# Graph attention layer: accumulating transfers for residual and x sum, x asked for a unit ahead, and ScalarE comparing from a PSUM copy of the s1 row with 13 of 16 chunks

## The chip, the cores and the metric

The kernel runs on one core of a Trainium2 chip. The engines meant below are TensorE (PE; its weight loads are PEld), VectorE (DVE), ScalarE (ACT), GpSimd (POOL) and SyncE (SP, which here only issues transfers). The metric is the device time of one execution in microseconds (us).

## The reference

One layer of graph attention over 8 graphs of 2048 nodes, with 8 heads of 64 features, then a residual and a layer norm. x is (8, 2048, 512), adj is (8, 2048, 2048) of 0 and 1.

```python
h = einsum('bnf,hfo->bhno', x, W)
s1 = einsum('bhno,ho->bhn', h, a1);  s2 = einsum('bhno,ho->bhn', h, a2)
e = leaky_relu(s1[..., :, None] + s2[..., None, :], negative_slope=0.2)
attn = softmax(where(adj > 0, e, -9e15), axis=-1)
out = layernorm(x + concat_heads(attn @ h), axis=-1)
```

## The kernel before

exp(leaky_relu(s1+s2)) is a product of a factor of the row and one of the column on each side of zero. So a head's attention for 512 rows needs two 0/1 masks, "edge and s1+s2 > 0" (`m_pos`) and "edge and not above 0" (`m_neg`), each multiplied with h times a column factor, split into a high and a low fp16 part.

**Batch and unit.** A batch (`b`, 8 of them) is one graph. It begins with a stage of 16 chunks: PE computes h for 128 columns (L426, fp32), DVE scales and splits it (L679 to L684, in `split_chunk`), and POOL subtracts to get the low parts (L892, L894). PE may be four chunks ahead, one per bank of `H_BANKS`. Then come 32 units: blocks of 512 rows (`k`, 4) by heads (`h`, 8). A unit is 4 x (1 + 32) positive and 4 x 32 negative matmuls of 65 columns (L442 to L446, L466, L467).

**How a unit's masks come about.** SP spreads the unit's s1 row over all partitions (`load_s1`, L264). The comparisons with the 16 chunks of s2 are written to `step`: ACT makes 12 (L504, `compare`), reading the row in SBUF, DVE 4 (L693, `DVE_SLOTS`). A `step` half is single, so ACT may write a half for unit u+1 only when DVE has taken that half of unit u (`pos_made`). DVE makes `m_pos` (L708) and `m_neg` (L717), two instructions each. On DVE the order in unit u is: largest |x| of an x tile, masks of unit u+1, extra work, `take_unit(u)` (L561 to L566, which waits for PE), a part of the layer norm.

**The next batch's x.** Half of the units (`TILE_UNIT` 0, 1, 3, 4, ... 22) handle an x tile of the next batch: SP loads it (`load_x`, L283), PE transposes it (L368), ACT copies it (L484), DVE takes the maximum (L552), POOL adds it to `x_sum` (L828). Load and use stand in the same unit. adj pieces are loaded, cut to fp8 on ACT (L478) and transposed by transfer. In units 24 to 30 PE and DVE make the next batch's scores, maxima and the small mean term.

**Output.** POOL scales each unit's result into `att` (L849, L854). After a block it adds `att` to `y`, which SP loaded with x (`residual`, L862), and DVE normalises in the next block's units 1 to 3 (`ln_first_half`, `ln_statistics`, `ln_apply`). There is one `y`.

The order on each engine is the written order of its block; semaphores are the only links.

Of the kernel before, what the change touches and what calls it, by code (L numbers as in the profile page):

```python
# [42 lines left out]
DVE_SLOTS = {0: (6, 7), 1: (6, 7)}  # L43
# [17 lines left out]
def gat_kernel(nc, x, adj, W, a1, a2, out):  # L61
# [25 lines left out]
    with ExitStack() as ctx:  # L87
# [19 lines left out]
        BANK_SUM = 5  # L107
# [19 lines left out]
        att = sb("att", [P, IT, H * O], F32)  # L127
        y = sb("y", [P, IT, F], F32)
# [46 lines left out]
        y_loaded = sem("y_loaded")  # L175
        s1_stored = sem("s1_stored")
        s1_loaded = [sem(f"s1_loaded{i}") for i in range(2)]
        out_stored = sem("out_stored", free=0)
# [13 lines left out]
        x_summed = sem("x_summed", free=2)  # L192
# [17 lines left out]
        lo_made = sem("lo_made", free=1)  # L210
        x_sum_turned = sem("x_sum_turned")
# [6 lines left out]
        r_row_made = sem("r_row_made")  # L218
        step_act = sem("step_act", free=QUADS)
# [10 lines left out]
        y_made = sem("y_made", free=0)  # L230
# [27 lines left out]
        def _(sp):  # L258
# [20 lines left out]
            def load_x(xi, slot, pair):  # L279
                sp.wait_ge(x_turned, at(x_turned, xi - 1))  # L280
                sp.wait_ge(x_maxed, at(x_maxed, xi - 1))
                sp.wait_ge(x_summed, at(x_summed, xi - 1))
                sp.dma_start(x_in[slot][:], x_tiles[bass.ds(pair, 1), slot].rearrange("a p f -> (a p) f")  # L283
                             ).then_inc(x_loaded[slot], 16)
# [7 lines left out]
            def store_block(g):  # L292
                sp.wait_ge(y_normed, g + 1)
                sp.dma_start(out_blocks[bass.ds((g + NBLK) % NBLK, 1)].rearrange("a p c f -> (a p) c f"),
                             y[:].rearrange("p (c e) f -> p c (e f)", e=2)).then_inc(out_stored, 16)
# [4 lines left out]
            for i in range(JC):  # L300
                if i == 2:
# [3 lines left out]
                    for n, a in enumerate((a1, a2)):  # L305
                        sp.dma_start(att[:, n, :], a.rearrange("h o -> (h o)").partition_broadcast(P)
                                     ).then_inc(a_loaded, 16)
# [12 lines left out]
            with sp.Fori(0, B) as b:  # L320
                for k in range(KB):
                    g = b * KB + k
                    for h in range(H):
                        unit = k * H + h
                        u = g * H + h
                        if unit == UNITS - 2:
                            sp.wait_ge(s1_stored, 16 * KB * (b + 2))
                        load_s1(u + 2, h % 2)
                        for i in cuts_of(k, h)[0] + cuts_of(k, h)[1]:
# [6 lines left out]
                        if unit in TILE_UNIT:  # L336
                            t = TILE_UNIT.index(unit)
                            load_x(JC * (b + 1) + t, t % 2, ((b + 1) * (JC // 2) + t // 2) % (NBLK * IT // 2))
                        if unit == STURN_UNIT + 1:
                            store_s1(b + 1)  # L340
                        if h == 5:
                            if k:
                                store_block(g - 1)
                            else:
                                with sp.If(b > 0):
                                    store_block(g - 1)
                        if h == 6:
                            sp.wait_ge(w_abs_summed, 1)
                            sp.wait_ge(out_stored, at(out_stored, 16 * g))
                            sp.dma_start(y[:].rearrange("p (c e) f -> p c (e f)", e=2),  # L350
                                         x_blocks[bass.ds(g, 1)].rearrange("a p c f -> (a p) c f")
                                         ).then_inc(y_loaded, 16)
            store_block(NBLK - 1)
# [9 lines left out]
        def _(pe):  # L363
# [8 lines left out]
            def turn_x_sum(n):  # L372
                pe.wait_ge(x_summed, at(x_summed, JC * (n + 1)))
# [34 lines left out]
            for fc in range(FC):  # L408
                mm = pe.matmul(ps[:, 0, :], ones[:], y[:, fc, :], start=(fc == 0), stop=(fc == FC - 1))
# [7 lines left out]
            with pe.Fori(0, B) as b:  # L417
                for jc in range(JC):
                    if jc == 2:
                        pe.wait_ge(s_col_copied, b + 1)  # L420
                    if jc == 3:
                        pe.wait_ge(tiny_step, 6 * b + 1)
                    if jc >= 4:
                        pe.wait_ge(hi_d_made, b * JC + jc - 3)
# [524 lines left out]
```

## Time and profile before

| | us |
|---|---|
| median of 3 runs (3199.03 to 3208.34) | 3201.51 |
| the profiled execution | 3208.02 |
| its span, first to last instruction | 3206.2 |
| PE busy | 2753.7 |
| DVE busy | 2742.4 |
| ACT busy | 2247.7 |
| POOL busy | 970.0 |

The mean granted TensorE clock is 0.969 of full speed. A batch takes some 390 us: 322 us for its 32 units and 69 us from the end of one batch's units to the next batch's first. PE's busy time is modelled; instructions overlap by some 0.1 us on DVE and ACT, so a mean duration is longer than the step from one instruction to the next. "issue" as a releaser means that nothing in the profile explains the wait.

### The profile page before, as it was taken

Reading aid. Unit: us, or ns where it says so; the run is one execution under the profiler, and the core shown is the slowest. Engines: PE = TensorE matmul, PEld = TensorE weight load, DVE = VectorE, ACT = ScalarE, POOL = GpSimd, SP = SyncE. Lnnn points to the kernel's source line nnn. Section 1 sums busy time; section 2 is a strip of 40 time slices with the busy share of each in tenths; the row PEclk is TensorE's granted clock in tenths of the full one; section 3 lists DMA queues with packets and bytes.
Section 4 is the critical chain, followed back from the end, with each engine's and each line's share of the span. In section 5 each row is a group of like instructions: output and inputs, shape, how many; then the busy total and the mean of one; then the engine's idle time right before and its main releaser. Section 6 shows DMA issues by size and latency. Waiting matters only on the chain.

```text
span 3206.2 us, 157311 instructions
## 1 busy us (share of the span) xinstructions
PE 2753.7 (86%) x68636; PEld 2400.1 (75%) x68636; DVE 2742.4 (86%) x4210; ACT 2247.7 (70%) x3517; POOL 970.0 (30%) x1043
## 2 busy tenths in 40 slices
PE   5898899888898889988998879998799978998887
PEld 2487776878678786788857878587785878758786
DVE  4898888988889888898888989888897988889887
ACT  2488873878648886488855878468773878738885
POOL 2522216222252223422243221532216222162221
PEclk9899999999999999999999999999999999999998
DMA  5335442444414545144442545325442344423443
GB/s 158 83 96 135 123 112 70 112 131 127 130 52 118 134 123 140 38 131 120 118 134 62 133 115 127 104 79 137 122 122 80 97 128 129 109 81 109 132 126 102
DMA packets 262958, 359.19 MB, mean 112 GB/s; under 512 B 159808, under 2 KB 159808, under 8 KB 262240
## 3 DMA queue, kind: packets, MB, share of 16 engines
q1 hardware_dynamic: 262240, 348.80, 40.5%
q8 instruction: 551, 9.03, 1.2%
q14 instruction: 167, 1.37, 0.2%
HBM read 279.97 MB, written 34.14 MB: 98 GB/s over the span
## 4 chain that ended last, share of the span: by engine, by line
PE 35%; DVE 24%; issue 17%; DMA 9%; ACT 7%; SPq 5%; POOL 1%; DVEq 0%; ACTq 0%; POOLq 0%
PE ps L426 12%; DVE step L693 11%; DMA x_in<-in_x 9%; ACT step L504 7%; PE ps L445 5%; PE ps L446 5%; PE ps L467 5%; PE ps L466 5%; DVE m_neg L717 3%; SPq L276 3%; DVE m_pos L708 2%; DVE y L589 2%; DVE total L564 1%; DVE neg_part L561 1%; SPq L269 1%
## 5 line engine op out<-in xcount | busy, mean ns | idle before, releaser
L504 ACT ACTIVATE step<-s_bc,s_steep 128x512 fp8e4<-128x512 f32 x3072 | 1916.9, 714 | 558.9 <-DVE m_pos L708 479.8
L445 PE MATMUL ps<-b_hi,m_pos 128*128 128x65 f16 x16384 | 1095.7, 196 | 22.8 <-issue 22.2
L446 PE MATMUL ps<-b_lo,m_pos 128*128 128x65 f16 x16384 | 1095.0, 195 | 18.7 <-issue 18.0
L467 PE MATMUL ps<-d_lo,m_neg 128*128 128x65 f16 x16384 | 1054.7, 194 | 33.5 <-issue 33.4
L445 PEld LDWEIGHTS ps<-b_hi,m_pos 128*128 128x128 fp8e5 x16384 | 1063.0, 99 | 24.6 <-issue 24.4
L446 PEld LDWEIGHTS ps<-b_lo,m_pos 128*128 128x128 fp8e5 x16384 | 1062.6, 99 | 25.1 <-issue 24.3
L466 PE MATMUL ps<-d_hi,m_neg 128*128 128x65 f16 x16384 | 1054.9, 194 | 27.8 <-issue 27.3
L466 PEld LDWEIGHTS ps<-d_hi,m_neg 128*128 128x128 fp8e5 x16384 | 1028.4, 98 | 62.8 <-issue 61.6
L467 PEld LDWEIGHTS ps<-d_lo,m_neg 128*128 128x128 fp8e5 x16384 | 1023.2, 98 | 19.4 <-issue 17.5
L708 DVE TENSOR_TENSOR m_pos<-step,maskT 128x1024 uint32<-128x1024 uint32 x512 | 642.8, 1294 | 63.1 <-ACT step L504 30.5
L693 DVE TENSOR_SCALAR step<-s_bc,s_neg 128x512 fp8e5<-128x512 f32 x1024 | 601.3, 650 | 6.4 <-DVE s_neg L652 3.2
L717 DVE TENSOR_TENSOR m_neg<-m_pos,maskT 128x1024 uint32<-128x1024 uint32 x512 | 603.4, 1219 | 0.0
L426 PE MATMUL ps<-W_sb,xT 128*128 128x512 f32 x1024 | 467.1, 619 | 47.9 <-DVE prod_d L684 26.4
L828 POOL TENSOR_TENSOR x_sum<-x_sum,x_in 128x512 f32<-128x512 f32 x144 | 185.6, 1289 | 886.8 <-DMA x_in<-in_x 886.7
L426 PEld LDWEIGHTS ps<-W_sb,xT 128*128 128x128 f32 x1024 | 202.0, 199 | 307.3 <-issue 272.9
L849 POOL TENSOR_TENSOR den_scaled<-den_inv,bound 128x4 f32<-128x4 f32 x256 | 81.6, 319 | 898.7 <-DVE den_inv L566 821.9
L442 PE MATMUL ps<-tiny,ones_bf 128*128 128x65 bf16 x1024 | 201.1, 196 | 175.9 <-DVE m_pos L708 153.1
L478 ACT ACTIVATE adj_cut<-adj_in 128x1024 fp8e4<-128x1024 int32 x264 | 272.4, 1046 | 101.7 <-DMA adj_in<-in_adj 101.7
L484 ACT ACTIVATE xT<-ps 128x512 f32<-128x512 f32 x144 | 83.4, 579 | 241.0 <-PE ps L368 241.0
L442 PEld LDWEIGHTS ps<-tiny,ones_bf 128*128 128x128 bf16 x1024 | 101.0, 99 | 195.6 <-DVE m_pos L708 166.5
L552 DVE TENSOR_REDUCE xmax<-x_in 128x1 f32<-128x512 f32 x144 | 98.0, 681 | 163.1 <-DMA x_in<-in_x 162.8
L561 DVE TENSOR_TENSOR neg_part<-ps,r_row 128x260 f32<-128x260 f32 x256 | 108.5, 424 | 122.5 <-PE ps L467 120.9
(79 smaller groups left out, 1841.8 us busy)
## 6 DMA issues: line engine op xcount, KB each, us to landing
adj_in<-in_adj SPq DMA_DIRECT2D x266, 512.0 KB, 4.4
s_bc<-s_rows SPq DMA_DIRECT2D x258, 256.0 KB, 3.4
x_in<-in_x SPq DMA_DIRECT2D x144, 256.0 KB, 4.4
y<-in_x SPq DMA_DIRECT2D x32, 1024.0 KB, 7.1
out<-y SPq DMA_DIRECT2D x32, 1024.0 KB, 7.1
maskT<-adj_cut SPq DMA_TRANSPOSE x264, 3.7
W_sb<-in_L_gnn_W SPq DMA_DIRECT2D x4, 256.0 KB, 6.6
s_rows<-sT SPq DMA_DIRECT2D x36, 16.0 KB
```

Of the source, the lines that this page charges most:

```text
L426: mm = pe.matmul(ps[:, H_BANKS[jc % 4], :], xT[:, fc, jc * P:(jc + 1) * P], W_sb[:, fc, :], start=(fc == 0), stop=(fc == FC - 1))
L442: pe.matmul(acc, ones_bf[:], tiny[:, h, :], start=True, stop=False)
L445: pe.matmul(acc, mask, b_hi[:, j, h, :], start=False, stop=False)
L446: mm = pe.matmul(acc, mask, b_lo[:, j, h, :], start=False, stop=(j == JC - 1))
L466: pe.matmul(acc, mask, d_hi[:, j, h, :], start=(j == 0), stop=False)
L467: mm = pe.matmul(acc, mask, d_lo[:, j, h, :], start=False, stop=(j == JC - 1))
L478: nc.scalar.activation(adj_cut8[slot][:], adj_in[slot][:], ACT.Relu, scale=STEEP, saturate=False).then_inc(adj_cut, 1)
L504: ins = nc.scalar.activation(chunk(step[qd], c, 0, BLK), s1_bc[h % 2][:], ACT.Relu, bias=s2_steep[:, j, h:h + 1], scale=STEEP, saturate=False)
L693: ins = V.tensor_scalar(chunk(step[qd], c, 0, BLK).bitcast(FP8_WIDE), s1_bc[hp][:], s2_neg[:, j, h:h + 1], STEP_UP, ALU.is_gt, ALU.mult, s ...
L708: V.tensor_tensor(words(m_pos[hp][:, js, :]), words(step[qd][:]), words(mask[:, js, :]), ALU.bitwise_and).then_inc(pos_made, 1)
L717: V.tensor_tensor(words(m_neg[hp][:, js, :]), words(m_pos[hp][:, js, :]), words(mask[:, js, :]), ALU.bitwise_xor).then_inc(neg_made, 1)
L828: G.tensor_tensor(x_sum[:], x_sum[:], x_in[slot][:], ALU.add).then_inc(x_summed, 1)
```

## The change

- ACT copies each unit's s1 row into PSUM bank 5 (new wait for its own earlier comparisons, then for the copy) and its comparisons read that bank. DVE makes 3 of 16 chunks, ACT 13.
- Bank 5 is no longer free for the stage: `H_BANKS` has three banks, and PE may be three chunks ahead.
- x tiles are asked for one unit before their use (`LOAD_UNIT`), and DVE's maximum comes after the masks, not before. The tile of unit 0 is transposed before that unit's positive matmuls.
- `x_sum` and the residual are formed by accumulating transfers that POOL issues (in the first batch's setup POOL still adds). `att` and the load of `y` are gone; there are two `y`.
- A batch's last block is normalised in the next batch's stage (behind chunks 11, 12, 14) and stored at unit 2.
- Unit 0's positive matmuls wait for the last chunk's low part only at the last mask of their first group. The loops carry `hint_back_edge`.

```diff
-DVE_SLOTS = {0: (6, 7), 1: (6, 7)}
+DVE_SLOTS = {0: (6, 7), 1: (7,)}
+    LOAD_UNIT = [max(v - 1, 0) for v in TILE_UNIT]
-    H_BANKS = (6, 5, 7, 4)
+    H_BANKS = (7, 4, 6)
...
             def compare(u, h, nth):
                 act.wait_ge(s1_loaded[h % 2], 16 * (nth + 1))
+                act.sem_inc(waited[act.engine], 1)
+                act.wait_ge(step_act, at(step_act, QUADS * u))
+                nc.scalar.activation(ps[:, BANK_S1, :], s1_bc[h % 2][:], ACT.Copy).then_inc(s1_copied, 1)
+                act.wait_ge(s1_copied, u + 1)
...
-                            ins = nc.scalar.activation(chunk(step[qd], c, 0, BLK), s1_bc[h % 2][:], ACT.Relu,
+                            ins = nc.scalar.activation(chunk(step[qd], c, 0, BLK), ps[:, BANK_S1, :], ACT.Relu,
...
-            with dve.Fori(0, B) as b:
+            with nc.Fori(0, B, engines=[dve.engine], hint_back_edge=True) as b:
...
+                    for when, work in ((11, ln_first_half), (12, ln_statistics), (14, ln_apply)):
+                        if jc == when:
+                            with dve.If(b > 0):
+                                work(KB * b - 1, 1)
...
-                        if unit in TILE_UNIT:
-                            max_x(...)
...
                             make_masks(u + 1, h + 1, maskT[k % 2], g * (H // 2) + (h + 1) // 2)
+                        if unit in TILE_UNIT:
+                            max_x(...)
...
+            def add_x(xi, t, odd, pair):
+                if t > 0:
+                    pool.wait_ge(x_summed, 16 * xi)
+                G.dma_start(x_sum[:], x_tiles[bass.ds(pair, 1), odd].rearrange("a p f -> (a p) f"),
+                            accum_op=ALU.add).then_inc(x_summed, 16)
...
-            def residual(g):
-                pool.wait_ge(y_loaded, 16 * (g + 1))
+            def residual(g, par):
                 pool.wait_ge(att_made, at(att_made, UNITS // KB * (g + 1)))
-                for half in range(2):
-                    t = slice(half * IT // 2, (half + 1) * IT // 2)
-                    G.tensor_tensor(y[:, t, :], y[:, t, :], att[:, t, :], ALU.add).then_inc(y_made, 1)
+                G.dma_start(y[par][:].rearrange("p (c e) f -> p c (e f)", e=2),
+                            x_blocks[bass.ds((g + NBLK) % NBLK, 1)].rearrange("a p c f -> (a p) c f"),
+                            accum_op=ALU.add).then_inc(y_made, 16)
```

## Rows read from the trace of the kernel before

**Rows 1.** The page: busy time by engine; the chain that ended last by engine

```profile
PE 2753.7 (86%) x68636; PEld 2400.1 (75%) x68636; DVE 2742.4 (86%) x4210; ACT 2247.7 (70%) x3517; POOL 970.0 (30%) x1043
...
PE 35%; DVE 24%; issue 17%; DMA 9%; ACT 7%; SPq 5%; POOL 1%; DVEq 0%; ACTq 0%; POOLq 0%
```

**Rows 2.** Busy by window: stretch, length, engines (instructions), PE clock, DMA share, GB/s

```profile
917.30:1239.30 322.00, 280.62 (x8436) 271.35 (x8436) 281.67 (x427) 247.99 (x392) 78.28 (x93) 0.98 0.43 115
1239.30:1308.30 69.00, 60.17 (x130) 25.84 (x129) 55.98 (x92) 30.49 (x44) 40.32 (x36) 0.92 0.36 93
930.90:1227.70 296.80, 255.51 (x7648) 246.34 (x7645) 265.50 (x399) 246.83 (x389) 66.58 (x80) 0.98 0.46 123
```

**Rows 3.** Waits in 930.9 to 1227.7: who for whom, total us, times, longest

```profile
ACT step L504 <- DVE m_pos L708: 58.3, 21, 9.3
...
PE ps L442 <- DVE m_pos L708: 22.5, 13, 5.0
...
DVE xmax L552 <- DMA x_in<-in_x: 18.1, 9, 5.1
...
POOL stat_all L840 <- issue: 14.0, 1, 14.0
```

**Rows 4.** Groups on ACT, 930.9 to 1227.7: busy us, mean ns, idle before

```profile
L504 ACT ACTIVATE step<-s_bc,s_steep 128x512 fp8e4<-128x512 f32 x348 | 217.1, 713 | 58.3 <-DVE m_pos L708 58.3
L478 ACT ACTIVATE adj_cut<-adj_in 128x1024 fp8e4<-128x1024 int32 x24 | 24.8, 1043 | 0.0
L484 ACT ACTIVATE xT<-ps 128x512 f32<-128x512 f32 x15 | 8.6, 576 | 0.0
...
L492 ACT ACTIVATE e_b<-s_rel 128x128 f32<-128x128 f32 x1 | 0.3, 299 | 0.0
```

**Rows 5.** Groups on DVE, 930.9 to 1227.7, columns as before

```profile
L708 DVE TENSOR_TENSOR m_pos<-step,maskT 128x1024 uint32<-128x1024 uint32 x58 | 73.2, 1302 | 3.9 <-DVE step L693 0.2
...
L693 DVE TENSOR_SCALAR step<-s_bc,s_neg 128x512 fp8e5<-128x512 f32 x116 | 68.2, 651 | 0.4
```

**Rows 6.** DVE in order of time: start, length, what, count, wait before

```profile
925.87 0.43 DVE L561 TENSOR_TENSOR neg_part<-ps,r_row 128x260 f32<-128x260 f32 x1 [8.26 <-PE ps L467]
...
934.34 0.43 DVE L561 TENSOR_TENSOR neg_part<-ps,r_row 128x260 f32<-128x260 f32 x1
...
936.67 1.66 DVE L693 TENSOR_SCALAR step<-s_bc,s_neg 128x512 fp8e5<-128x512 f32 x4
...
954.43 2.21 DVE L589 TENSOR_SCALAR y<-y,ln_mv,ln_rstd 128x512 f32<-128x512 f32 x4
...
1079.52 6.45 DVE L693 TENSOR_SCALAR step<-s_bc,s_neg 128x512 fp8e5<-128x512 f32 x4
```

**Rows 7.** ACT in order of time

```profile
930.98 7.49 ACT L504 ACTIVATE step<-s_bc,s_steep 128x512 fp8e4<-128x512 f32 x12 [8.40 <-DVE m_pos L708]
...
1239.31 7.48 ACT L504 ACTIVATE step<-s_bc,s_steep 128x512 fp8e4<-128x512 f32 x12 [11.05 <-DVE s_neg L652]
```

**Rows 8.** A DVE wait of the whole run; the stage's last two chunks on DVE

```profile
DVE r_row L657 <- issue: 31.0, 7, 4.8
...
1302.12 0.69 DVE L679 TENSOR_TENSOR b_hi<-ps,k_b 128x512 f16<-128x512 f32 x1 [0.95 <-PE ps L426]
...
1305.55 0.69 DVE L679 TENSOR_TENSOR b_hi<-ps,k_b 128x512 f16<-128x512 f32 x1 [0.95 <-PE ps L426]
```

**Rows 9.** PE in order of time: chunk 4's start; unit 0's start

```profile
1261.05 1.22 PE L426 MATMUL ps<-W_sb,xT 128*128 128x512 f32 x1 [2.95 <-DVE prod_d L684]
...
1308.32 0.22 PE L442 MATMUL ps<-tiny,ones_bf 128*128 128x65 bf16 x1 [2.81 <-POOL b_lo L892]
```

**Rows 10.** Transfers by line, last figure issue to landing (us); the end on POOL and DVE

```profile
y<-in_x SPq DMA_DIRECT2D x32, 1024.0 KB, 7.1
...
3191.96 4.63 POOL L862 TENSOR_TENSOR y<-y,att 128x1024 f32<-128x1024 f32 x2
...
3196.63 1.29 DVE L576 BATCH_NORM_STATS2 ln_stats<-y 128x6 f32<-128x512 f32 x2 [1.01 <-POOL y L862]
```

More of the change, by code:

```diff
@@ L126, in gat_kernel @@
         wa = sb("wa", [P, FC, 32], F32)
-        att = sb("att", [P, IT, H * O], F32)
-        y = sb("y", [P, IT, F], F32)
+        y = [sb(f"y{i}", [P, IT, F], F32) for i in range(2)]
         sT = sb("sT", [P, BLK], F32)
@@ L210, in gat_kernel @@
         lo_made = sem("lo_made", free=1)
+        x_added = sem("x_added", free=2)
         x_sum_turned = sem("x_sum_turned")
@@ L318, in _ @@
             load_s1(1, 1)
-            with sp.Fori(0, B) as b:
+            with nc.Fori(0, B, engines=[sp.engine], hint_back_edge=True) as b:
                 for k in range(KB):
@@ L325, in _ @@
                         u = g * H + h
+                        if unit == 2:
+                            with sp.If(b > 0):
+                                store_block(g - 1, 1)
                         if unit == UNITS - 2:
@@ L328, in _ @@
                         load_s1(u + 2, h % 2)
+                        for t in range(JC):
+                            if LOAD_UNIT[t] == unit == 0:
+                                load_x(JC * (b + 1) + t, t % 2, ((b + 1) * (JC // 2) + t // 2) % (NBLK * IT // 2))
                         for i in cuts_of(k, h)[0] + cuts_of(k, h)[1]:
@@ L408, in _ @@
             for fc in range(FC):
-                mm = pe.matmul(ps[:, 0, :], ones[:], y[:, fc, :], start=(fc == 0), stop=(fc == FC - 1))
+                mm = pe.matmul(ps[:, 0, :], ones[:], y[0][:, fc, :], start=(fc == 0), stop=(fc == FC - 1))
             mm.then_inc(w_abs_summed, 1)
@@ L443, in _ @@
                             for j in range(JC):
+                                if unit == 0 and it == 0 and j == JC - 1:
+                                    pe.wait_ge(lo_made, at(lo_made, 2 * JC * (b + 1) - 1))
+                                    pe.sem_inc(waited[pe.engine], 1)
                                 mask = chunk(m_pos[hp], j, it * P, P).bitcast(FP8_WIDE)
@@ L449, in _ @@
                             pe.wait_ge(lo_made, at(lo_made, 2 * JC * (b + 1)))
-                        if unit in TILE_UNIT:
+                        if unit and unit in TILE_UNIT:
                             t = TILE_UNIT.index(unit)
@@ L518, in _ @@
             compare(0, 0, 0)
-            with act.Fori(0, B) as b:
+            with nc.Fori(0, B, engines=[act.engine], hint_back_edge=True) as b:
                 for k in range(KB):
@@ L809, in _ @@
                         for when, work in ((1, ln_first_half), (2, ln_statistics), (3, ln_apply)):
-                            if h == when:
-                                if k:
-                                    work(g - 1)
-                                else:
-                                    with dve.If(b > 0):
-                                        work(g - 1)
-            ln_first_half(NBLK - 1)
-            ln_statistics(NBLK - 1)
-            ln_apply(NBLK - 1)
+                            if h == when and k:
+                                work(g - 1, (k - 1) % 2)
+            ln_first_half(NBLK - 1, 1)
+            ln_statistics(NBLK - 1, 1)
+            ln_apply(NBLK - 1, 1)
         @block.gpsimd
@@ L887, in _ @@
                 G.tensor_copy(bound[:], bound_next[:]).then_inc(bound_taken, 1)
+                with pool.If(b > 0):
+                    residual(KB * b - 1, 1)
                 for jc in range(JC):
```

136 lines of the change are left out of this document (65 added, 71 removed).

## The prediction, made before the changed kernel had run

> **What bounds the kernel now.** I read the page first, then busy time by window, the waits of one stretch, the groups on each engine there, and the engines in order of time. The page [rows 1] names no single bound: PE and DVE are both busy for 86% of the span, ACT for 70%, and the chain passes through PE, DVE, "issue", transfers and ACT. So one has to go by stretch. In the batch that I looked at, the units take 322 us and the way from the last unit to the next batch's first unit 69 us [rows 2]. I take this batch for all eight.
>
> Inside the units I took 930.9 to 1227.7, from the first comparison of unit 3 to the last of unit 31: 29 units in 296.8 us, 10.2 us each. DVE is busy for 265.5 of them, PE for 255.5, ACT for 246.8 [rows 2]. DVE's idle time is mostly 18.1 us of waiting for an x tile; PE waits 22.5 us for `m_pos`, and ACT waits 58.3 us for DVE to take a `step` half [rows 3]. So both others wait for DVE, and DVE waits for x. DVE bounds the units. It also runs slowly there: four chunks of `step` take 1.66 us when POOL is quiet and 6.45 us while POOL adds a residual and an x tile [rows 6]; over the stretch a chunk costs 68.2/116 = 0.59 us against 0.41.
>
> **The change, part by part.** I go engine by engine over the 29 units.
>
> DVE: 29 chunks fewer and the rest at about 0.45 us (POOL keeps its two small operations a unit): 87 x 0.45 = 39 for 68.2 [rows 5], so -29. `m_pos` comes down from 73.2 to 58 x 1.14 = 66.5 (1.14 is the step of undisturbed ones), -6.5. The layer norm of block 3 moves to the stage, about -5. The x waits, 18.1, go: the tile is asked for a unit (9 us or more) earlier, and is looked at after the masks. DVE's work comes to 265.5 - 40.5 = 225 us.
>
> PE: nothing is removed. Two takes that follow PE directly are 8.47 us apart [rows 6], in units with a tile; its busy time of 255.5 is what it needs.
>
> ACT: what does a comparison from PSUM cost? No row has one. A cut of 1024 elements from SBUF takes 1.043 us, an exponential of 128 takes 0.299 [rows 4]: 0.83 ns an element and 0.19 fixed, so 0.619 for 512. The copy of an x tile from PSUM, 512 elements, takes 0.576, or 0.04 less. A comparison takes 0.713 (it has a bias column), and 12 take 7.49 [rows 7], a step of (7.49 - 0.713)/11 = 0.616. Bounds: 0.616 if PSUM gives nothing, 0.576 if it gives those 0.04. I take 0.576, since the copy of x is the nearest row that reads PSUM.
>
> The new copy of s1 has 0.62 at most as its own length (same size, from SBUF); it can't overlap the comparison before it, and the next one waits for it: I take 0.75, bounds 0.6 and 1.0. It is free only while ACT would have waited for DVE anyway; that cover (58.3 us now) is what the faster DVE takes away. So I count it whole. Per unit: 13 x 0.576 + 0.75 = 8.24 us, against 7.39 now. Over the stretch: 29 x 8.24 = 239.0; 24 cuts at a step of 0.95, 22.8; 14 copies of x at 0.48, 6.7; scores and exponentials, 1.1. Sum 269.6 us. ACT becomes the bound, with PE (255.5) close behind and DVE (225) clear.
>
> Does ACT ever wait for DVE then? Count from the end of a unit's comparisons. DVE does the second `m_pos` and both `m_neg` (3.5 us), at worst a maximum (0.6), the take (1.05), the longest piece of layer norm (2.2, [rows 6]), three chunks (1.3 to 1.6) and the next first `m_pos` (1.2): done at about 10.2 us. ACT needs it for the unit after next, at 9.3 us plus cut and copy, so 11. It just fits. PE has lumps in units 24 to 27 (scores and mean, some 9 us together) and random stops. I add 5 us of lost time, bounds 0 and 20. The stretch: 274.6 for 296.8, so **-22.2 us a batch**.
>
> Before the stretch, comparison 3 waits for `m_pos` of unit 2. DVE comes to it 0.6 (maximum moved) and 0.4 (one chunk) sooner: -1.0. Behind it, ACT waits for the next batch's s2 the 11.05 us wait of [rows 7]; there the copy comes after that wait, +0.75.
>
> The boundary. DVE starts the next batch 4.7 us after its last instruction with "issue" as the reason, 31.0 us in seven times [rows 8]: it is the loop's way back. I take it that the hint removes it: -31 in all, bounds -31 and 0. It is on the path, since PE's fifth chunk waits for DVE's first [rows 9]. The three banks make PE wait for that same event with three chunks done, not four. PE needs 3.43 a chunk (DVE's last two chunks, both waiting for PE, start that far apart, [rows 8]), DVE 2.4 (four operations, each 0.6 to the next) plus its inserts; following both through the 16 chunks, with 5.4 us of layer norm now behind chunks 11, 12 and 14, DVE ends 48.4 us after its first chunk, where it now ends 46.9 (1261.05 to 1305.55 plus 2.4, [rows 8, 9]). So +1.5. Unit 0 no longer waits for the last low part before its first matmul (2.81 us idle, [rows 9]) but some 1 us into it: -1.4. Together nil, bounds -2 and +4.
>
> The transfers. A plain load of 1 MB lands in 7.1 us [rows 10]. The residual is issued after the take of unit 7, and DVE first reads it two units of some 9.4 us later: hidden, and dearer only if it takes over 18. The one place without cover is the end: POOL's addition starts at 3191.96, DVE's second half follows at 3196.63 and ends at 3197.9 [rows 10]. With 8.1 us for the transfer (7.1 and about 1 for issuing it) and 2.5 us for both halves that becomes 3202.4: +4.5. POOL's additions of x (hidden now) become issues, at no cost as long as POOL keeps a unit ahead of DVE.
>
> The Trainium skill has a rule against this (SBUF — State Buffer, Who interferes with whom): VectorE in a two-port mode locks GpSimd out of the shared port pair for the whole instruction, and only transfers that GpSimd issues suffer, since it must write their descriptors. The trace shows the same lock from the other side (6.45 for 1.66 us, above). By that rule the new transfers start later, by about one VectorE instruction; the 18 us of cover make that nothing in the sum.
>
> **Sum**, against the profiled execution of 3208.0: 8 x (-22.2 - 1.0) = -185.6; 7 x 0.75 = +5.3; -31; +4.5. That is -206.8, so 3001 us; the median stands 6.5 us below the profiled execution, so **2995 us**.
>
> **Rivals.**
> 1. PSUM saves nothing on a comparison. For: the one row that reads PSUM on ACT has another form, no bias column and a wide output. Then a step is 0.616, 29 x 13 x 0.04 = +15.1 a batch, 121 in all: 3116 us.
> 2. The three engines don't interlock as neatly: ACT goes on waiting for DVE or PE, 20 us a batch and not 5. For: it fits by only 1 us in the worst unit, and now it waits 58.3. Against: DVE gets 40 us lighter. 8 x 15 = +120: 3115 us.
> 3. ACT reads PSUM faster than I take it, and PE is the bound: the stretch falls to PE's 255.5 plus 5, -14 a batch: 2883 us. For it a comparison would have to step at about 0.54.
> 4. Slower than before: POOL is held at each transfer. It now stands idle for 14.0 us without a releaser ahead of its one odd instruction, the reduction over partitions [rows 3], so a change of kind of work can be dear there. If each of the 16 tile transfers cost it 14, it would need 16 x 15 + 8 x 1 = 248 us for 24 units in which ACT needs about 24 x 9.4 = 226, and with a like price for the way back (28 a transfer) 472 us: +246 a batch, about 4960 us. `take_unit` waits for POOL's result of two units before, so there is one unit of cover and no more. It decides from a hold of (226 - 24)/16 = 12.6 us a transfer, and the whole gain is lost from 26 us a batch more, at 14.3.
> 5. The change doesn't do what it says: the hint leaves the way back at 4.4 us. 3026 us.
>
> **From cases to numbers.** Forecast and its small variants 0.50 (2940 to 3060), rival 5 by itself 0.10, rival 1 0.13, rival 2 0.12, both together 0.03 (3116 + 120 = 3236), rival 3 0.06, rival 4 0.06. A measurement of this kernel can tell about 0.3% from no change. Slower: rival 4 but for a hold near 14 us (0.05), and most of the two together (0.02), 0.07. Same: what is left of these, 0.02. Faster: the rest, 0.91. The range leaves out rival 3, rival 4, the two together, and some edges of the others: 2925 to 3125.
>
> **What would show each step.** ACT busy for over 90% of the units, its waits for `m_pos` under 10 us in a stretch of 29 units, and the step of a comparison 0.576: the ACT term. Chunks on DVE at about 0.45 us, no wait of the maximum on x: the DVE term. The wait of L657 gone: the hint. First chunk to last split 48 us: the stage. DVE's statistics waiting for `y` only at the end: the transfers' cover. It is wrong if a comparison from PSUM costs 0.61 or more, or if DVE waits for POOL's results.

## The result, and the profile after

The changed kernel took 3148.4 us (median, 3138.4 to 3158.8) against 3200.3 (3190.6 to 3208.3) for the kernel before on the same chip: a ratio of 0.983, 95% interval 0.981 to 0.986. It is faster, by 52 us (1.7%) and not by the 205 of the forecast, and lies outside the range.

The page after, beside [rows 1]: busy time by engine, the chain that ended last by engine, and two rows of the DMA queues, GpSimd's (q0) and that of TensorE's instructions (q8) (queue, kind: packets, MB, share of 16 engines).

```profile
PE 2744.1 (87%) x68636; PEld 2398.0 (76%) x68636; DVE 2522.8 (80%) x3954; ACT 2419.3 (77%) x4029; POOL 827.5 (26%) x1011
...
q0 software_dynamic: 27136, 67.12, 12.7%
q8 instruction: 545, 8.93, 1.2%
...
PE 67%; issue 13%; DVE 10%; ACT 7%; DMA 1%; SPq 1%; POOL 0%; DVEq 0%; ACTq 0%; POOLq 0%
```

TensorE now carries the chain, with 67% for 35%; ScalarE, forecast as the bound, has 7%. Below is the batch of [rows 2]: its units, its boundary, and the 29 units from comparison 3 to comparison 31 (same columns).

```profile
892.06:1208.97 316.91, 279.15 (x8432) 270.01 (x8432) 254.32 (x393) 267.71 (x452) 59.03 (x88) 0.98 0.55 126
1208.97:1275.05 66.08, 58.28 (x132) 25.62 (x133) 56.52 (x96) 32.22 (x50) 41.22 (x35) 0.95 0.45 112
907.00:1197.20 290.20, 254.94 (x7670) 246.14 (x7669) 235.43 (x358) 265.76 (x446) 50.84 (x76) 0.98 0.58 131
```

The 29 units take 290.2 us for 296.8; 274.6 had been forecast. DVE lost 30 us of work (forecast 40), ACT took on 19 (forecast 23), and PE's 255 stayed. So PE was idle for 35.3 us (290.2 - 254.9), before for 41.3. What it waited for has changed. First the groups on PE in this stretch after, then in [rows 3]'s stretch before (busy us, mean ns, idle ahead of them, releaser):

```profile
L455 PE MATMUL ps<-b_lo,m_pos 128*128 128x65 f16 x1856 | 124.0, 195 | 12.2 <-issue 12.0
L454 PE MATMUL ps<-b_hi,m_pos 128*128 128x65 f16 x1856 | 124.0, 195 | 7.1 <-issue 7.1
L476 PE MATMUL ps<-d_lo,m_neg 128*128 128x65 f16 x1866 | 121.3, 195 | 7.1 <-issue 7.0
L475 PE MATMUL ps<-d_hi,m_neg 128*128 128x65 f16 x1866 | 121.1, 195 | 6.8 <-issue 6.7
L448 PE MATMUL ps<-tiny,ones_bf 128*128 128x65 bf16 x116 | 22.5, 194 | 2.1 <-issue 2.1
```

```profile
L445 PE MATMUL ps<-b_hi,m_pos 128*128 128x65 f16 x1856 | 125.1, 196 | 3.0 <-issue 2.9
L446 PE MATMUL ps<-b_lo,m_pos 128*128 128x65 f16 x1856 | 125.0, 196 | 0.5 <-issue 0.5
L466 PE MATMUL ps<-d_hi,m_neg 128*128 128x65 f16 x1856 | 117.8, 193 | 4.0 <-issue 3.9
L467 PE MATMUL ps<-d_lo,m_neg 128*128 128x65 f16 x1856 | 117.8, 194 | 1.4 <-issue 1.4
L442 PE MATMUL ps<-tiny,ones_bf 128*128 128x65 bf16 x116 | 22.9, 197 | 22.7 <-DVE m_pos L708 22.5
L368 PE MATMUL ps<-ident,x_in 128*128 128x128 f32 x56 | 8.9, 282 | 9.1 <-DMA x_in<-in_x 9.1
```

The idle time ahead of L442 and L368, nearly all waits for `m_pos` and for x, was 31.8 us. Ahead of the same two matmuls after (L448, and L368 with 0.0) it is 2.1, none of it for either. But the idle time inside the runs of matmuls, where nothing of the kernel is waited for, went from 8.9 to 33.2 us. I call these stops. Over the whole run the page gives them, as idle time ahead of the four mask matmul lines, as 102.8 us before and 260.1 after. With "issue" as the reason it is 100.9 and 235.2. Of the rest, in the changed kernel and all built on it, 17.4 us or so is unit 0's wait for its last low part, which in the kernel before stands ahead of L442. Two stops, in order of time, and two of the transfers that were issued, by GpSimd, some 10 us ahead of the first:

```profile
967.76 1.24 POOL L882 DMA_DIRECT2D y<-in_x  x1 [0.99 <-POOL y L876]
968.67 1.27 POOL L849 DMA_DIRECT2D x_sum<-in_x  x1
...
978.95 0.20 PE L475 MATMUL ps<-d_hi,m_neg 128*128 128x65 f16 x1 [2.23 <-issue]
...
1025.34 0.20 PE L455 MATMUL ps<-b_lo,m_pos 128*128 128x65 f16 x1 [3.12 <-issue]
```

What is waited for there is TensorE's own code. Its queue moved 8.93 MB in 545 packets of 16 KB (above), which is 65 bytes for each of its 2 x 68636 instructions, one packet for some 126 matmuls with their weight loads. The 27 stops over 0.25 us of this stretch are 126 or 127 matmuls apart, or a multiple of that, and over the run they come back at the same places of the loop's body: 13 places have one in at least seven of the eight batches. By the packet records each stop ends 1.2 to 1.6 us after the last such packet landed: the one at 1025.34 had its packet from 1022.94 to 1023.82, the one at 978.95 from 976.62 to 977.57. With no stop and at full clock PE runs through a packet's code in some 3.86 us. A packet takes about 1.0 to arrive and 1.4 more pass before PE goes on, so it has to start within some 1.45 us of PE's passing the boundary of the block before. With the boundaries laid out from the places of the stops, packets start about 1.4 us behind them in the kernel before, in the mean, and 1.9 in the changed one; some 205 of 512 start later than 1.45, and some 287 in the changed kernel.

The Trainium skill (Runtime: NRT & Kernel Launch, Instruction fetch mechanics) says that an engine's code comes in 16 KiB blocks of 256 instructions over a DMA queue of its own, the next one during the current one, at a cost that is mostly hidden. The block size agrees with these rows; the cost doesn't: 235 us of 3137 stand open.

Other rows answer to the prediction's steps. The groups of the comparison and of the DVE chunk in the stretch:

```profile
L519 ACT ACTIVATE step<-ps,s_steep 128x512 fp8e4<-128x512 f32 x377 | 221.4, 726 | 38.6 <-DVE m_pos L722 34.5 <-ACT ps L510 4.1
...
L707 DVE TENSOR_SCALAR step<-s_bc,s_neg 128x512 fp8e5<-128x512 f32 x87 | 43.8, 559 | 1.0 <-issue 0.3
```

In order of time, a unit's comparisons, and PE at the boundary (beside [rows 9]):

```profile
961.52 7.63 ACT L519 ACTIVATE step<-ps,s_steep 128x512 fp8e4<-128x512 f32 x13 [0.28 <-ACT ps L510]
...
1226.87 1.22 PE L429 MATMUL ps<-W_sb,xT 128*128 128x512 f32 x1 [7.24 <-DVE prod_d L698]
```

Waits of the whole run, then the residual's row among the issues:

```profile
DVE xmax L567 <- DMA x_in<-in_x: 25.5, 11, 7.3
...
DVE r_row L671 <- issue: 4.3, 7, 0.7
```

```profile
y<-in_x POOLq DMA_DIRECT2D x32, 1024.0 KB, 10.4
```

### The profile page after: what moved, and what is told of

It is laid out like the page before. It is cut to its first block, busy times and chain, and to the rows that moved or that the text cites. A ratio compares the mean times of both kernels' runs of the same rounds, so it can differ in the third digit from the quotient of the medians.

```text
span 3136.7 us, 158793 instructions
## 1 busy us (share of the span) xinstructions
PE 2744.1 (87%) x68636; PEld 2398.0 (76%) x68636; DVE 2522.8 (80%) x3954; ACT 2419.3 (77%) x4029; POOL 827.5 (26%) x1011
## 3 DMA queue, kind: packets, MB, share of 16 engines
q0 software_dynamic: 27136, 67.12, 12.7%
q8 instruction: 545, 8.93, 1.2%
## 4 chain that ended last, share of the span: by engine, by line
PE 67%; issue 13%; DVE 10%; ACT 7%; DMA 1%; SPq 1%; POOL 0%; DVEq 0%; ACTq 0%; POOLq 0%
PE ps L475 14%; PE ps L476 14%; PE ps L455 13%; PE ps L454 13%; PE ps L429 8%; ACT step L519 7%; PE ps L368 2%; DVE m_neg L731 1%; DVE y L603 1%; PE ps L386 1%; PE ps L399 1%; DVE prod L695 1%; PE ps L448 1%; DVE prod_d L698 1%; DVE m_pos L722 1%
## 5 line engine op out<-in xcount | busy, mean ns | idle before, releaser
L519 ACT ACTIVATE step<-ps,s_steep 128x512 fp8e4<-128x512 f32 x3328 | 1954.1, 726 | 289.7 <-DVE m_pos L722 246.9
L475 PE MATMUL ps<-d_hi,m_neg 128*128 128x65 f16 x16384 | 1071.9, 195 | 67.0 <-issue 61.2
L476 PE MATMUL ps<-d_lo,m_neg 128*128 128x65 f16 x16384 | 1072.7, 195 | 42.3 <-issue 42.1
L476 PEld LDWEIGHTS ps<-d_lo,m_neg 128*128 128x128 fp8e5 x16384 | 1039.1, 99 | 34.9 <-issue 33.3
L722 DVE TENSOR_TENSOR m_pos<-step,maskT 128x1024 uint32<-128x1024 uint32 x512 | 623.8, 1242 | 163.4 <-ACT step L519 130.6
L429 PE MATMUL ps<-W_sb,xT 128*128 128x512 f32 x1024 | 464.1, 615 | 61.5 <-DVE prod_d L698 54.7
L707 DVE TENSOR_SCALAR step<-s_bc,s_neg 128x512 fp8e5<-128x512 f32 x768 | 391.1, 565 | 12.4 <-DVE s_neg L666 3.6
L487 ACT ACTIVATE adj_cut<-adj_in 128x1024 fp8e4<-128x1024 int32 x264 | 291.1, 1132 | 120.0 <-DMA adj_in<-in_adj 120.0
L493 ACT ACTIVATE xT<-ps 128x512 f32<-128x512 f32 x144 | 96.9, 673 | 175.8 <-PE ps L368 175.8
L510 ACT ACTIVATE ps<-s_bc 128x512 f32<-128x512 f32 x256 | 174.6, 682 | 71.9 <-DVE s_neg L666 71.4
L876 POOL TENSOR_TENSOR y<-total,den_scaled 128x256 f32<-128x256 f32 x256 | 206.2, 805 | 22.7 <-POOL den_scaled L871 2.3
L448 PE MATMUL ps<-tiny,ones_bf 128*128 128x65 bf16 x1024 | 199.0, 194 | 11.2 <-issue 6.3
L917 POOL TENSOR_TENSOR d_lo<-prod_d,d_hi 128x512 f16<-128x512 f32 x128 | 176.2, 1376 | 9.0
## 6 DMA issues: line engine op xcount, KB each, us to landing
y<-in_x POOLq DMA_DIRECT2D x32, 1024.0 KB, 10.4
```

The lines of the kernel that those rows point to most:

```text
L429: mm = pe.matmul(ps[:, H_BANKS[jc % 3], :], xT[:, fc, jc * P:(jc + 1) * P], W_sb[:, fc, :], start=(fc == 0), stop=(fc == FC - 1))
L448: pe.matmul(acc, ones_bf[:], tiny[:, h, :], start=True, stop=False)
L475: pe.matmul(acc, mask, d_hi[:, j, h, :], start=(j == 0), stop=False)
L476: mm = pe.matmul(acc, mask, d_lo[:, j, h, :], start=False, stop=(j == JC - 1))
L487: nc.scalar.activation(adj_cut8[slot][:], adj_in[slot][:], ACT.Relu, scale=STEEP, saturate=False).then_inc(adj_cut, 1)
L519: ins = nc.scalar.activation(chunk(step[qd], c, 0, BLK), ps[:, BANK_S1, :], ACT.Relu, bias=s2_steep[:, j, h:h + 1], scale=STEEP, saturate= ...
```

## The experiments

Three numbers are given for each kernel: its time, as a ratio to the kernel before timed beside it (whose medians were 3193 to 3203); the stops, read from its page as above; and two stretches from the first matmul of a unit (L448) to another's, meaned over the batches: unit 3 to unit 31 (28 units), and unit 31 to the next batch's unit 3. Stops and stretches come from one execution of each kernel, and executions of one kernel differ by up to 38 us: the profile of a_extra_sp, c_split and c_best, for instance, is their slowest execution, that of the changed kernel and c_split_fine their fastest. The first experiments have the changed kernel as their base, those with b_ the kernel before, those with c_ the base named.

| kernel | median | ratio (95%) | stops | units | boundary |
|---|---|---|---|---|---|
| before | | 1 | 102.8 | 289.1 | 100.2 |
| after | 3148.4 | 0.983 (0.981, 0.986) | 260.1 | 278.1 | 101.9 |
| a_small_adj | 3045.8 | 0.954 (0.951, 0.957) | 99.4 | 263.9 | 104.1 |
| a_pool_sum | 3087.0 | 0.966 (0.960, 0.972) | 158.3 | 271.0 | 102.6 |
| a_extra_sp | 3123.6 | 0.972 (0.967, 0.978) | 223.5 | 277.8 | 102.2 |
| a_extra_pool | 3092.2 | 0.964 (0.962, 0.967) | 193.4 | 272.8 | 102.3 |
| a_sbuf_compare | 3152.8 | 0.988 (0.984, 0.991) | 270.4 | 280.9 | 101.1 |
| a_no_hint | 3134.3 | 0.979 (0.976, 0.982) | 258.8 | 275.7 | 106.1 |
| b_psum | 3208.6 | 1.004 (1.003, 1.006) | 81.6 | 284.9 | 105.7 |
| b_x_ahead | 3119.7 | 0.974 (0.972, 0.976) | 124.1 | 278.6 | 99.0 |
| b_x_psum | 3122.1 | 0.975 (0.973, 0.976) | 129.2 | 272.4 | 105.6 |
| b_x_hint | 3105.8 | 0.970 (0.967, 0.974) | 136.1 | 279.5 | 96.9 |
| b_banks3 | 3225.6 | 1.010 (1.007, 1.012) | 80.3 | 286.7 | 104.0 |
| c_fine_adj | 3080.7 | 0.963 (0.958, 0.969) | 133.1 | 268.7 | 104.2 |
| c_split | 3073.4 | 0.960 (0.957, 0.963) | 169.7 | 269.9 | 103.1 |
| c_split_sbuf | 3101.5 | 0.969 (0.966, 0.972) | 153.0 | 272.2 | 103.6 |
| c_split_fine | 3070.7 | 0.962 (0.957, 0.966) | 101.7 | 266.1 | 103.4 |
| c_ps_small_adj | 3048.9 | 0.953 (0.951, 0.955) | 87.4 | 265.5 | 103.9 |
| c_ps_small_sbuf | 3032.2 | 0.948 (0.946, 0.950) | 93.9 | 263.3 | 103.2 |
| c_best | 3080.5 | 0.963 (0.961, 0.966) | 139.9 | 271.5 | 101.9 |

**Is the code late because of the kernel's own transfers?** Of all data, the adj pieces are the most. The first experiment makes them small and leaves every instruction.

```diff
-                adj_in[slot][:], adj_tiles[..., slot * JH * P:(slot + 1) * JH * P]
+                adj_in[slot][:, 0:n], adj_tiles[..., slot * JH * P:slot * JH * P + n]   # n = 64 in the loop
```

In the loop the masks then come from stale columns.

> The changed kernel, but in the loop each adjacency transfer fetches 64 of 1024 columns (32 KB for 512 KB); the cut and transposed pieces are otherwise stale, so the masks are wrong in part. Theory 1 (TensorE's own code, which comes in 16 KB transfers over the same DMA engines, arrives late because data transfers are queued before it): TensorE's waits with the reason 'issue' inside the units, some 280 us in the changed kernel, fall under 140, and the time falls by 100 to 200 us, to 2950 to 3050. Theory 2 (TensorE at full pace outruns the delivery of its code whatever else is moved): the waits stay over 240 and the time within 40 us of 3148.

The stops fell to 99.4 us, and the ratio by 0.029, as the first theory had it. Two rows of its page, GpSimd's queue and the chain:

```profile
q0 software_dynamic: 27136, 67.12, 13.3%
...
ACT 41%; PE 29%; issue 16%; DVE 11%; DMA 1%; ACTq 1%; SPq 1%; POOL 1%; DVEq 0%; POOLq 0%
```

With the code in time ScalarE carries most of the chain (41%), as forecast, and the units take 25.2 us a batch less than before, where the prediction's stretch had 22.2. Units pass faster than in the changed kernel and the stops still go, so it is the traffic that makes them; pace alone does not. The cut on ScalarE also waited less for its pieces (78 us for 120), which is a part of the gain I can't separate.

A part of the gain comes through PE's clock. Two stretches of 127 matmuls in the changed kernel, the first between the stop that ends at 971.11 (1.92 us long) and the one that ends at 978.95, the second behind a stop of 0.60 us (columns of [rows 2]):

```profile
971.20:976.70 5.50, 5.50 (x127) 5.39 (x126) 1.48 (x2) 5.35 (x10) 0.00 (x0) 0.69 1.04 208
...
1018.20:1022.20 4.00, 4.00 (x127) 3.89 (x127) 3.41 (x8) 4.00 (x8) 0.86 (x2) 1.00 0.96 350
```

Behind the long stop PE runs partly at 1.2 GHz (granted clock 0.69 in the mean) and takes 5.5 us for what takes 4.0 at 2.4 GHz. It isn't so behind every stop: the one of 3.12 us at 1025.34 is not followed by it. Over the run the clock was 0.965 to 0.969 in the changed kernel's executions and 0.972 to 0.977 in those of a_small_adj, and PE's busy time for the same matmuls fell from 2744.1 to 2708.2 us. That is some 36 of the 93 to 103 us between the two. That the stops bring the clock down is not shown by itself.

**Which transfers of the change?** Its new kind is the accumulating one. The next kernel adds x on GpSimd again and leaves the residual's transfer as it is.

```diff
-                            add_x(JC * b + t, t, t % 2, ...)
+                            add_first_x(JC * (b + 1) + t, t % 2, (b + 1) * (JC // 2) + t // 2)
```

> The changed kernel with the x sum added up on GpSimd from the loaded tile, as before; the residual remains an accumulating transfer. Theory 1: 32 MB of 360 are no longer moved, so the waits for code fall by a tenth to a fifth and the time by 15 to 50 us. Theory 3 (it is the accumulating transfers of GpSimd's queue that hold the code up): 128 of 160 of them are gone, the waits fall by half and the time by 80 us or more. Theory 2: no change, or slower by up to 20 us since VectorE's comparisons run beside GpSimd's additions again.

Two more put the same 256 KB back beside it, without adding: once from SP, once from GpSimd.

```diff
+                            sp.dma_start(x_extra[:], x_tiles[...])       # a_extra_sp
+                            G.dma_start(x_extra[:], x_tiles[...])        # a_extra_pool
```

> a_pool_sum (sum of x on GpSimd's engine) with the 256 KB x tile loaded once more, as a plain transfer of SP's queues at the unit where the changed kernel accumulates it: the same bytes from memory as the changed kernel, no accumulation. If bytes in flight at the code's fetches count alone: back at 3140 to 3160, and TensorE's stops summed over the run back near 290 us. If the accumulating kind or the GpSimd queue counts: stays near a_pool_sum's 3087, within 15 us.

> The same extra 256 KB load, issued by GpSimd (its software-made queue), plain and not accumulating. If the queue of GpSimd is what holds the code up: near the changed kernel (3135 to 3160) while a_extra_sp stays low. If only accumulating transfers do: both stay near 3087. If bytes do: both near 3150.

a_pool_sum gains 55 us on the changed kernel (0.983 to 0.966) and its stops fall by 102; the time lies between what the two theories had said, 15 to 50 us and 80 or more. The same bytes from GpSimd's queue cost nothing that can be measured (0.964 beside 0.966), though the stops grow by 35 us. From SP's queue the ratio is 0.972, some 20 us more than a_pool_sum with intervals that touch, and 26 more than a_extra_pool; the stops grow by 65 us in its slowest execution, and neither number expected for it came (3123.6 us). So plain bytes count too, between nothing and some 40 us, and more from the queue of SP than from GpSimd's; why is open. The accumulating transfer costs 0.983 - 0.964, some 60 us, against the same bytes in the same queue: that part is the accumulation. The page shows what is different about it. First the row of a_extra_pool for this queue and for the transfer, then the changed kernel's row for the transfer:

```profile
q0 software_dynamic: 18944, 67.12, 9.4%
...
x_extra<-in_x POOLq DMA_DIRECT2D x128, 256.0 KB, 3.5
```

```profile
x_sum<-in_x POOLq DMA_DIRECT2D x128, 256.0 KB, 4.6
```

For the same 67.12 MB the queue's packets hold the engines for 12.7% of the span and not 9.4%; without either it is 6.0% (a_pool_sum). A tile's accumulation therefore takes the engines twice the time of a plain load (6.7 against 3.4 points) and lands in 4.6 us for 3.5 (the plain one of SP's queue, issued at another moment, in 4.5). The Trainium skill (DMA: Bandwidth & Descriptors, Issuing engines are not separate DMA queues) has all transfers interleaved on the same 16 engines whoever starts them. These runs agree: adj pieces from SP's queue and x tiles from GpSimd's both delay the packets of TensorE's code.

**Can the delivery be made milder?** Both from a_pool_sum: adj in four transfers of 256 columns each, and the residual in two of 512 KB, a unit apart, with the layer norm a unit later; c_split_fine has both.

```diff
+                for part in range(0, JH * P, JH * P // 4):                # c_fine_adj
+                    sp.dma_start(adj_in[slot][:, part:part + 256], ...)
-            residual(g, par)                                              # c_split
+            residual(g, par, half)    # y[par][:, 2 * half:2 * half + 2, :]
```

> a_pool_sum with each adj piece loaded in four transfers of 128 KB, so 1 KB of each row in place of 4 KB. If a code block of 16 KB waits behind single large packets in a queue, smaller packets let it through: 20 to 60 us less than 3087, TensorE's stops below 120 us. If it waits for bytes and not for packets: within 10 us of 3087; more issues on SP may even cost 5 to 20 us.

> a_pool_sum with the residual's accumulating transfer of 1 MB cut into two of 512 KB, a unit apart, and the normalization a unit later. If long accumulating transfers hold the code up: 10 to 25 us less than a_pool_sum. If the sum of accumulated bytes does: the same within 8 us.

> c_split with the adj pieces in four transfers of 128 KB each: both milder deliveries together. c_split stood at 3073 and c_fine_adj at 3081 against a_pool_sum's 3087. If shorter packets and shorter accumulations both count: 3055 to 3070. If the two differences were run-to-run spread: 3070 to 3090.

c_fine_adj took 25 us off the stops and 0.003 off the ratio, less than its interval and than the 20 us that would have told. c_split has the lowest ratio of the kernels that do the whole work, 0.960, but its interval touches a_pool_sum's, and its stops did not fall. Together they bring the stops to 101.7 and the units to 266.1 us, but that is the fastest of four executions (3056.7 to 3089.5) beside c_split's slowest, and the median is c_split's: this step stays unclear. All three beat both the kernel before and the changed one.

**Do adj and the accumulation act through the same stops?**

> a_pool_sum with each adj load in the batch loop cut from 512 KB to 32 KB (the masks are then made from stale columns; the work of the engines is unchanged): both known sources of the late code taken away. a_small_adj gained 103 us and a_pool_sum 61 over the changed kernel. If they act through the same stops of TensorE: 3010 to 3030, with the stops summed below 80 us. If the accumulating x_sum costs in another way than the code's delay: the two gains add in full, below 2990.

a_pool_sum with the small adj loads took 3048.9 us, where a_small_adj, which accumulates, took 3045.8. Neither number expected came (3010 to 3030, or below 2990). The accumulation costs 60 us with full adj loads and nothing with small ones, so the two don't add. That fits one path, the code's delay, with room for either alone. It fits as well that the engines themselves stand at 3030 to 3050 us and hide the rest: with stops at 87 to 99 us no kernel here was faster, and ScalarE, PE and VectorE share the chain. The runs don't part the two.

**What is comparing from PSUM worth?** Taken out of the changed kernel, whose stage keeps its three banks, and put alone into the kernel before:

```diff
-DVE_SLOTS = {0: (6, 7), 1: (7,)}                                        # a_sbuf_compare
+DVE_SLOTS = {0: (6, 7), 1: (6, 7)}
-                nc.scalar.activation(ps[:, BANK_S1, :], s1_bc[h % 2][:], ACT.Copy)
-                ... nc.scalar.activation(chunk(...), ps[:, BANK_S1, :], ACT.Relu, ...)
+                ... nc.scalar.activation(chunk(...), s1_bc[h % 2][:], ACT.Relu, ...)
```

> The changed kernel with comparisons from SBUF, no copy to PSUM, and 12 of 16 chunks on ScalarE, as before. If TensorE and its code bound the changed kernel (theories 1 to 3), the split of the chunks matters little: within 40 us of 3148. If ScalarE bounds it as I forecast, ScalarE loses 0.24 us a unit of work (8.24 to 7.39 plus nothing for the copy) and the kernel gets faster or stays; if VectorE is the nearer bound, it gets slower by 256 x 0.45 = 115 us.

> The kernel before with only this part of the change: s1 copied to PSUM, comparisons from there, 13 and 3 chunks, three banks in the stage. VectorE bounds the kernel before, and loses 0.59 us a unit: by that alone 256 x 0.59 = 150 us less, 3050. With theories 1 or 2, part of what TensorE no longer waits for VectorE comes back as waits for code: 40 to 100 us less, 3100 to 3160.

Neither showed a gain; b_psum missed both numbers and was slower by 13 us (0.004). Its granted clock was 0.961 to 0.966 (mean 0.964) where the kernel before beside it had 0.965 to 0.975 (mean 0.970), and PE was busy 16 us longer for the same matmuls (2770.1 for 2753.7). The late code might have hidden the gain, and in b_psum the waits for x. So x was asked for ahead in the kernel before, without and with it:

```diff
+    LOAD_UNIT = [max(v - 1, 0) for v in TILE_UNIT]
-                        if unit in TILE_UNIT: load_x(...)
+                            if LOAD_UNIT[t] == unit: load_x(...)         # and max_x after make_masks
```

> The kernel before with one part of the change: x tiles are asked for a unit ahead and VectorE takes their maximum after the masks; both sums still by accumulating on GpSimd's engine as before. If the waits for x (VectorE's 18 us in the stretch of rows 3) were the bound: some 70 to 110 us faster than before (3090 to 3130). If TensorE's pace is set by its own code arriving late (as the comparison of a_small_adj says), only the room that this leaves: 0 to 40 us faster (3150 to 3190).

> x asked for ahead and the compare from PSUM with 13 and 3 chunks, without the accumulating transfers, the two y tiles and the loop hint of VectorE's and GpSimd's loops. If ScalarE's compare was the next bound: 3000 to 3080. If the code delivery is, it stands at 3100 to 3170, and no slower than the changed kernel by more than 20 us, since it has fewer bytes in flight but no second y tile.

Asking for x ahead is worth 0.026, more than the whole change. That is the first of the two numbers expected (3090 to 3130): the waits for x were a bound, and late code took back little (stops 102.8 to 124.1). PSUM beside it is worth nothing in the time, but the table shows two halves: the units 6.2 us a batch shorter (278.6 to 272.4), the boundary 6.6 longer. The row copy takes a PSUM bank from the stage of projections, so that one edit was tried alone:

```diff
-    H_BANKS = (6, 5, 7, 4)
+    H_BANKS = (7, 4, 6)                                                  # b_banks3; waits moved to match
```

> The kernel before with one edit: the projections of the stage go through three PSUM banks in place of four (bank 5 left unused, as the row copy leaves it). From one tiny-row matmul of unit 31 to that of unit 3 of the next batch the kernel before takes 100.2 us and before + compare from PSUM 105.7. If the missing bank is what costs this, 30 to 50 us over the seven boundaries and the first: 3230 to 3250. If it is the row copy or ScalarE's longer compare in the stage: within 10 us of the kernel before.

31 us slower (30 to 50 expected), with the boundary 3.8 us longer and PE waiting for DVE there:

```profile
PE ps L426 <- DVE prod_d L684: 48.5, 8, 8.2
...
PE ps L426 <- DVE tiny_f L631: 5.3, 1, 5.3
```

The kernel before has 26.4 us in the first of these and none in the second; the changed kernel has 54.7 and 5.4. So the missing bank is 3.8 of the 5.5 us that b_psum adds at the boundary and of the 6.6 of b_x_psum, more than half of why the gain in the units doesn't show. And with the code in time?

> c_ps_small_adj with the compare back in SBUF (12 chunks on ScalarE, 4 on VectorE, no copy of the s1 row to PSUM). With the late code out of the way ScalarE's bound should show: if the compare from PSUM is worth what the prediction gave it (10 us a batch of 296.8 to 286 or less), this is 20 to 80 us slower than c_ps_small_adj. If TensorE's pace alone sets the units: within 10 us of it.

> c_split with the compare from SBUF, 12 and 4 chunks. In the changed kernel this part was worth 4 us and beside b_x_ahead nothing. If ScalarE becomes the bound as the stops get shorter: 10 to 30 us slower than c_split's 3073. If TensorE bounds: within 8 us.

> c_split_fine (sum of x on GpSimd, the residual accumulated in two halves, adj in four transfers) with the compare from SBUF again, 12 and 4 chunks, and the bank that this frees given back to the stage (four banks). If the compare from PSUM gains in the units what it costs in the stage: within 15 us of c_split_fine's 3071. If the fourth bank gives back 5 us a batch and ScalarE isn't the bound: 3030 to 3055. If ScalarE's SBUF compare bounds as in c_split_sbuf: 3065 to 3085.

c_ps_small_sbuf came out 17 us faster than its twin with PSUM, on the other side of what was expected. The chains by engine of c_ps_small_adj, then of c_ps_small_sbuf:

```profile
PE 32%; ACT 31%; DVE 17%; issue 16%; DMA 1%; ACTq 1%; SPq 1%; POOL 0%; DVEq 0%; POOLq 0%
```

```profile
DVE 33%; PE 31%; issue 21%; ACT 9%; DMA 1%; DVEq 1%; POOL 0%; ACTq 0%; POOLq 0%; SPq 0%
```

From PSUM, ScalarE's unit is 7.63 us for 13 chunks and about 1 for the copy and the wait behind it, against 7.5 for 12 from SBUF. The change moves 0.5 us off DVE and puts 1.1 on ScalarE; it trades one bound for another of much the same size. Yet c_split_sbuf was 28 us slower than c_split. A part of that came with a lower clock (0.962 to 0.968 for 0.970 to 0.972, PE busy for 2747.3 us and not 2725.3); why PE had less of it there, and why the order turns, is open. c_best, with the fourth bank back, took 1.7 us a batch off the boundary of c_split_sbuf, and with the finer adj some 17 us off its time (0.969 to 0.963), but was not better than c_split_fine.

**The loop's way back.**

```diff
-            with nc.Fori(0, B, engines=[...], hint_back_edge=True) as b:
+            with nc.Fori(0, B, engines=[...], hint_back_edge=False) as b:    # a_no_hint; the reverse in b_x_hint
```

> The changed kernel with the back edge of every engine's loop unhinted. The kernel before lost 31.0 us at seven returns of VectorE's loop (rows 8). If the hint gives them back: 3170 to 3185, about 20 to 35 us more than the changed kernel. If TensorE's late code decides and the returns were cover for something else: within 10 us of the changed kernel's 3148.

> b_x_ahead (the kernel before with x asked a unit ahead) with all five loops hinted, still with plain loads of the residual and one y tile, still comparing from SBUF, 12 and 4 chunks. If the hint is worth what the kernel before lost at the returns: 3088 to 3100. It would then stand beside a_pool_sum, and the second y tile, the accumulating residual and the compare from PSUM together would be worth nothing.

The boundary is 4.2 us longer without the hint, and DVE's wait at the way back is 31.5 us in seven times again, for 4.3 with it; on b_x_ahead the hint makes the boundary 2.1 shorter. In time b_x_hint is 13 us better, with intervals that touch, and just misses what was expected. a_no_hint, expected at 3170 to 3185 or within 10 us of 3148, is no worse than the changed kernel (3134.3; 0.979 and 0.983): its units are 2.4 us a batch shorter. The mechanism is there; its worth, between nothing and some 13 us, is under what these runs resolve.

## Why the prediction was wrong

The forecast took 206.8 us off the profiled execution of 3208.0; the profiled execution after is 3138.4, so 69.6. The 137 us between them lie in two places, but for 2 us at the end of the run.

**The units, about 98.** I had -22.2 and -1.0 a batch, 23.2; measured is 289.1 - 278.1 = 11.0, so 12.2 too much, eight times. The step that failed is "random stops. I add 5 us of lost time, bounds 0 and 20", and with it "ACT becomes the bound". The lost time, ScalarE's 290.2 - 265.8 us of idling in the stretch, was 24.4 us and not 5. In the profile of before the stops were there to be read: 102.8 us ahead of four lines, each with "issue" as the reason. I took them for noise, asked neither what they were nor what the change would do to them. They went from 8.9 to 33.2 us in the stretch. Two things raise them. With the waits for x gone they grow a little (b_x_ahead: 102.8 to 124.1); I read this as PE having less slack in which a late block can land unseen. And the accumulating transfers, which I had priced only by their own landing, take time of the engines on which the code comes (158.3 to 260.1 in the changed kernel; the same bytes without accumulation, 193.4 or 223.5). With the accumulation removed 55 to 60 us of time come back, with the adj traffic some 93, and a_small_adj then has the forecast's gain in the units, a part of it through the clock. Between the kernel before and the changed one the clock hardly differs (0.969 and 0.967), so it isn't what the forecast missed; but PE's 255.5 us of a stretch, which I took for "what it needs", were not its least.

**The boundary, about 37.** I had the banks and the layer norm at +1.5, unit 0's earlier start at -1.4, the copy at +0.75 and the hint at -4.4, so -3.6 for each of seven. Measured is +1.7 (100.2 to 101.9), 5.3 off. The bank term was mis-sized: I had +1.5 with the layer norm, b_banks3 gives 3.8 without it. I followed the sixteen chunks only on DVE, from its first split to its last (forecast 48.4 us; measured from the first `prod_d` to the last 51.5, before 47.1). PE, one bank shorter, now stands for 7.24 us where it stood for 2.95 [rows 9]. The end of the run, from the last unit's first matmul, took 6.4 us more, forecast 4.5.

Point by point: a comparison steps at (7.63 - 0.726)/12 = 0.575 us, forecast 0.576, so rival 1 is out. The row copy steps at 0.98 (it starts at 970.37, the next comparison at 971.35), forecast 0.75, at the upper bound: 29 x 0.23 = 6.7 us of ScalarE's time in the stretch. ACT is busy for 92% of the stretch, forecast over 90%, but waits 34.5 us for `m_pos` where under 10 had been named. A chunk on DVE is 0.50 us (43.8/87), forecast 0.45. The maximum waits for x no more in the stretch, 25.5 us in all for 162.8. DVE's wait of 31.0 us at the way back is 4.3: the hint does what it says. DVE's statistics wait for `y` once, for 10.4 us at the end; the residual lands in 10.4 us and was hidden elsewhere, as taken, from DVE but not from PE. Of the rivals, 2 came nearest (3115, "ACT goes on waiting"), for a reason it did not have: the third party was not an engine but a transfer of code. Rival 4 came only in a size that costs nothing: over the run GpSimd stands without a releaser for 5.4 us in 27 times ahead of the tile transfers and for 40.8 in 15 ahead of the residual's, 4.8 at most, where 12.6 at each of the tiles would have decided. Its 13.6 us ahead of the reduction are as before.

## What to carry to other kernels

Read idle time with no releaser inside a run of equal instructions as a cost of its own, by line and over the whole run, before pricing a change that lets that engine run faster or adds transfers: here it grew by some 135 us while the named waits fell. This unrolled TensorE stream fetched its code over the DMA engines that carry the data, so a transfer's price includes the code that it delays; an accumulating one took the engines twice the time of a plain one, and a sum on an idle GpSimd can be the better place. And when a change takes a shared thing such as a PSUM bank, time the stage that gave it up alone. When a kernel's time moves, look at the granted clock of its executions before you explain the rest.

## What the runs showed of the hardware

- A 16 KB block of TensorE's code that came late ended the stop 1.2 to 1.6 us after it landed; the engine used a block up in 3.86 us at full clock.
- 127 matmuls behind a stop of 1.92 us took 5.5 us at a mean granted clock of 0.69, others 4.0 at 1.00; behind a stop of 3.12 us the clock did not fall.
- 128 accumulating tile transfers of 256 KB took 6.7% of 16 DMA engines' span, plain ones of the same queue 3.4%.
- A 1 MB accumulating transfer landed in 10.4 us, a plain one of the kernel before in 7.1 [rows 10]; halved, 7.3 each (c_split).
- ScalarE's comparison steps at 0.575 us from PSUM and 0.616 from SBUF [rows 7] (512 elements, bias column); its row copy into PSUM took 0.60 to 0.70, and the next comparison started 0.28 after it.
